# Dividing by the softmax sums after the product with the values, in the last cross attention

## Chip, core and metric

The kernel runs on one core of one Trainium2 chip. The metric is the device time of one execution in microseconds, a median over runs. TensorE (PE in the rows, PEld its weight loads), VectorE (DVE), ScalarE (ACT), GpSimd (POOL) and SyncE (SP) run their own instruction streams and meet through semaphores.

## The reference, cut to what matters

Thirty-two batches of 112 rows of 256 go through four stages: a cross attention, a self attention with routed experts, a second cross attention, and a linear layer on quantised rows. Every stage adds to the residual x. The change lies in the third stage, and the fourth is interleaved with it:

```python
    scale = d ** (-0.5)                      # h, d = 8, 64
    q = (x @ Wq).reshape(B, Sq, h, d).transpose(0, 2, 1, 3)
    k = (context @ Wk).reshape(B, -1, h, d).transpose(0, 2, 1, 3)
    v = (context @ Wv).reshape(B, -1, h, d).transpose(0, 2, 1, 3)
    scores = jnp.einsum('bhid,bhjd->bhij', q, k) * scale
    attn = jax.nn.softmax(scores, axis=-1)
    out = jnp.einsum('bhij,bhjd->bhid', attn, v)
    out = out.transpose(0, 2, 1, 3).reshape(B, Sq, h * d)
    return out @ Wo + bo
...
    x = x + _L1_xattn_ref(_layernorm(x, axis=-1), ctx_768, L1_xattn_Wq, L1_xattn_Wk, L1_xattn_Wv, L1_xattn_Wo, L1_xattn_bo)
    x = x + _L1_ffn_ref(_layernorm(x, axis=-1), L1_ffn_weight, L1_ffn_bias)
```

The context has 375 keys of 192. The softmax divides each row of exponentials by its sum. The linear layer (_L1_ffn_ref) quantises x in blocks of 32 to a small grid before its product.

## The kernel before

The last stage is the function cross_last. It holds one instruction stream per engine, each written as a function step(b, par) that over_batches calls for b from a little below 0 to a little above 31: the first few steps and the last ones are written out, the middle ones are a loop of two steps per turn (TensorE: steps 6 to 29). The order inside a step is written by hand. What an engine does in one step belongs to several batches; `exists` leaves out those that are not there at the two ends.

The eight heads of a batch are four units of two heads. TensorE's step b does, in this order: transposes of the quantised rows xd of batch b-3 (L1984, into a bank of quad) and of the normalised rows xn of batch b+1 (L1984, into proj); scores of units 0 and 1 of batch b (L102); the out product of batch b-2 (L1989, reads oT) and the last linear product of batch b-3 (L1994), both into proj; the transposes of the probabilities of unit 2 of batch b-1 (L108); the query product of batch b+1 (L1969), into the bank that the second head of unit 0's scores held, so that it waits for that unit's exponentials; transposes of unit 3; scores of units 3 and 2; the product of the probabilities with the values of batch b-1 (L114, 48 matrix products of 64 columns of v, output in psum out); then key and value products for the next batches (L182), with the transposes of units 0 and 1 of batch b between them.

VectorE's step b takes the negated maxima of batch b+1 (dve_max, L119) as scores come, adds proj to the residual for batch b-1 (L1899) and to the final rows for batch b-2 (L1910), normalises the four units of probabilities of batch b+1 (dve_normalise, L122 and L126: a reciprocal of two sums, then one multiplication for each of the two heads; units 1 and 0 in mid-step, 3 and 2 at its end), mixes the experts' rows in (L1869), applies the norms (L169), and quantises batch b-1 in twelve instructions from L1302 to L1317, of which the last writes xd.

ScalarE takes exponentials with their sums (act_exp, L134), copies transposed probabilities out of PSUM (act_spread, L130), and copies queries, keys, values, and psum out into oT (L1809). GpSimd subtracts the rounded halves of q, k and the context (L1705, L1708, L1724, L1729, L1735), fetches experts' rows, and computes the norms' powers.

Of the kernel before, what the change touches and what calls it, by code (L numbers as in the profile page):

```python
# [79 lines left out]
class Core:  # L80


    def __init__(self, nc, ctx, name, psum, units, keys, chunk, vdim):
        self.keys, self.chunk, self.chunks, self.vdim = keys, chunk, keys // chunk, vdim
        self.out = psum["out"]
        self.scores = [t[0:T, :, 0:keys] for t in psum["scores"]]
        self.score_sums = [t[0:T, :, 0:keys + 1] for t in psum["scores"]]
        self.turned = psum["turned"][0:chunk, :, 0:self.chunks * T]
        sb = lambda n, shape: ctx.enter_context(nc.sbuf_tensor(f"{name}_{n}", shape, F32))
        sem = lambda n: ctx.enter_context(nc.semaphore(f"{name}_{n}"))  # L90
        self.negmax, self.sums, self.recip = (sb(n, [T, units, 2]) for n in ("negmax", "sums", "recip"))
        self.probs = [sb(f"probs{i}", [T, 2, keys]) for i in range(units)]
        self.probsT = [sb(f"probsT{i}", [chunk, 2, self.chunks, T]) for i in range(units)]
        self.scores_ready, self.max_ready, self.exp_ready = sem("scores_ready"), sem("max_ready"), sem("exp_ready")
        self.recip_ready, self.probs_ready, self.turned_ready = sem("recip_ready"), sem("probs_ready"), sem("turned_ready")
        self.spread_act, self.values_ready = sem("spread_act"), sem("values_ready")
# [24 lines left out]
    def dve_normalise(self, dve, u, done):  # L121
        dve.reciprocal(self.recip[:, u, :], self.sums[:, u, :]).then_inc(self.recip_ready, 1)  # L122
        dve.wait_ge(self.recip_ready, done)
        for j in range(2):
            p = self.probs[u][:, j, :]
            last = dve.tensor_scalar(p, p, self.recip[:, u, j:j + 1], None, ALU.mult)  # L126
        last.then_inc(self.probs_ready, 1)
# [1420 lines left out]
def cross_last(nc, mem, ctx_t, w, residual, out):  # L1548
# [5 lines left out]
    with ExitStack() as ctx:  # L1554
# [70 lines left out]
        def emit(block):  # L1625
# [116 lines left out]
            def _(act):  # L1742
# [3 lines left out]
                def step(b, par):  # L1746
# [11 lines left out]
                    if exists(b):  # L1758
                        act.wait_ge(core.max_ready, 4 * b + 1)
                        wait(act, core.turned_ready, 4 * b - 3)  # L1760
                        core.act_exp(act, 0)
# [20 lines left out]
                    if exists(b):  # L1782
                        act.wait_ge(core.max_ready, 4 * b + 3)
                        wait(act, core.turned_ready, 4 * b)
                        core.act_exp(act, 3)
                    if exists(b + 1):
                        act.wait_ge(k_mm, 4 * b + 5)
                        wait(act, k_ready, 4 * b + 1)
                        act.activation(kT[:, 0, :], psum["turned"][:, 1, :][:, 0:CTXE], ACT.Copy).then_inc(k_whole, 1)
# [16 lines left out]
                    if exists(b - 1):  # L1806
                        act.wait_ge(core.values_ready, 4 * b)
                        wait(act, op_mm, b - 1)
                        act.activation(oT[:, :, :].rearrange("p k t -> p (k t)"), psum["out"][:, 0:4 * T], ACT.Copy).then_inc(o_ready, 1)  # L1809
# [40 lines left out]
            def _(dve):  # L1850
# [37 lines left out]
                def step(b, par):  # L1888
# [14 lines left out]
                    if exists(b + 1):  # L1903
                        dve.wait_ge(core.exp_ready, 4 * b + 6)
                        core.dve_normalise(dve, 1, 4 * b + 5)
# [11 lines left out]
                    if exists(b + 1):  # L1917
                        dve.wait_ge(core.exp_ready, 4 * b + 5)
                        core.dve_normalise(dve, 0, 4 * b + 6)
# [5 lines left out]
                    if exists(b + 3):  # L1925
                        wait(dve, xT_mm, b + 3)
                        norm.dve_apply(dve, b + 3, xn[:, :], row(residual, b + 3))
                    if exists(b - 1):
                        quantise(b - 1, 0)
# [7 lines left out]
                    if exists(b + 1):  # L1937
                        dve.wait_ge(core.exp_ready, 4 * b + 7)
                        core.dve_normalise(dve, 3, 4 * b + 7)
                    if exists(b + 1):  # L1940
                        dve.wait_ge(core.exp_ready, 4 * b + 8)
                        core.dve_normalise(dve, 2, 4 * b + 8)
# [4 lines left out]
            def _(pe):  # L1947
# [49 lines left out]
                def step(b, par):  # L1997
# [67 lines left out]
                    if exists(b - 1):  # L2065
                        pe.wait_ge(core.probs_ready, 4 * b)
# [22 lines left out]
                    if exists(b - 1):  # L2089
                        pe.wait_ge(core.probs_ready, 4 * b - 1)  # L2090
# [54 lines left out]
                    if exists(b - 1):  # L2145
                        pe.wait_ge(core.spread_act, 4 * b)
                        pe.wait_ge(v_ready, 3 * b)
                        core.pe_values(pe, 3, v_of(1 - par))
                    if exists(b + 1):
# [13 lines left out]
                    if exists(b):  # L2163
# [13 lines left out]
                        elif exists(b + 1):  # L2177
                            wait(pe, xT_ready, b + 2)
                        v_product(proj, par, 2)
# [12 lines left out]
                    if exists(b):  # L2192
                        pe.wait_ge(core.probs_ready, 4 * b + 2)
# [25 lines left out]
                    if exists(b):  # L2219
                        pe.wait_ge(core.probs_ready, 4 * b + 1)  # L2220
# [101 lines left out]
```

## Time and profile before

| | us |
|---|---|
| median of 3 runs (1954.52 to 1957.32) | 1955.18 |
| the profiled execution, its own time | 1952.96 |
| its span, first to last instruction | 1951.1 |
| TensorE busy | 1865.6 |
| VectorE busy | 1493.8 |
| ScalarE busy | 1270.0 |
| GpSimd busy | 952.1 |

The span is what the trace covers; 1.9 us of the execution's time lie around it. Busy times are sums over all stages, so the table ranks the engines but doesn't say which of them a given stage waits for. The last stage takes the span from about 1282 us on, some 20 us a batch.

### The profile page before, as it was taken

Reading aid. Unit: us, or ns where it says so; the run is one execution under the profiler, and the core shown is the slowest. Engines: PE = TensorE matmul, PEld = TensorE weight load, DVE = VectorE, ACT = ScalarE, POOL = GpSimd, SP = SyncE. Lnnn points to the kernel's source line nnn. Section 1 sums busy time; section 2 is a strip of 40 time slices with the busy share of each in tenths; the row PEclk is TensorE's granted clock in tenths of the full one; section 3 lists DMA queues with packets and bytes.
Section 4 is the critical chain, followed back from the end, with each engine's and each line's share of the span. In section 5 each row is a group of like instructions: output and inputs, shape, how many; then the busy total and the mean of one; then the engine's idle time right before and its main releaser. Section 6 shows DMA issues by size and latency. Waiting matters only on the chain.

```text
span 1951.1 us, 61515 instructions
## 1 busy us (share of the span) xinstructions
PE 1865.6 (96%) x20887; PEld 1637.1 (84%) x20887; DVE 1493.8 (77%) x3438; ACT 1270.0 (65%) x2720; POOL 952.1 (49%) x1616
## 2 busy tenths in 40 slices
PE   6999999999899999789999999969999999999996
PEld 5888888888678888689999999958888888888885
DVE  6778888788478788766666666657888888888886
ACT  2555555555477777557777777747777677777773
POOL 4556555664256676630000000066767677676751
PEclk8999999999899999899999999979999999999998
DMA  8222233222051111275555655422111111111100
GB/s 238 90 89 88 88 111 95 88 88 63 22 165 33 35 38 40 65 260 190 205 196 188 199 203 189 137 81 60 32 41 35 40 35 40 35 34 38 32 15 10
DMA packets 116595, 182.05 MB, mean 93 GB/s; under 512 B 10850, under 2 KB 94562, under 8 KB 116066
## 3 DMA queue, kind: packets, MB, share of 16 engines
q1 hardware_dynamic: 110386, 166.51, 26.7%
q0 software_dynamic: 6144, 14.69, 2.5%
q8 instruction: 40, 0.66, 0.1%
q14 instruction: 25, 0.20, 0.0%
HBM read 127.68 MB, written 53.48 MB: 93 GB/s over the span
## 4 chain that ended last, share of the span: by engine, by line
PE 52%; DVE 2%; issue 1%; DMA 1%; POOL 1%; ACT 1%; ACTq 0%; SPq 0%; DVEq 0%; POOLq 0%
PE ps_quad L1518 11%; PE ps_out L1538 9%; PE ps_quad L182 6%; PE ps_quad L102 4%; PE ps_out L114 4%; PE ps_turned L108 4%; PE ps_quad L1969 3%; PE ps_proj L1989 3%; PE ps_turned L182 3%; PE ps_proj L182 2%; PE ps_proj L1994 1%; PE ps_proj L1526 1%; DVE c_negmax L119 1%; ACT c_probs L134 0%; DMA c_wv<-in_L_xattn_Wv 0%
## 5 line engine op out<-in xcount | busy, mean ns | idle before, releaser
L1518 PE MATMUL ps_quad<-e_xT,w 128*128 128x128 f32 x2016 | 235.3, 275 | 1.7 <-DVE e_xT L1476 1.7
L1518 PEld LDWEIGHTS ps_quad<-e_xT,w 128*128 128x128 f32 x2016 | 230.4, 192 | 2.2 <-DVE e_xT L1476 2.2
L369 ACT ACTIVATE a_probsT<-ps_quad 125x1792 f32<-125x1792 f32 x96 | 159.9, 1666 | 99.4 <-PE ps_quad L549 99.4
L1658 POOL TENSOR_TENSOR c_held<-minus_half 1x1 f32<-1x1 f32 x32 | 9.5, 298 | 407.9 <-DMA slots<-e_y 405.4
L1433 ACT ACTIVATE e_act_T<-ps_quad,fc_b 128x128 f32<-128x128 f32 x504 | 137.3, 384 | 91.4 <-PE ps_quad L1518 91.3
L134 ACT ACTIVATE c_probs<-ps_quad,c_negmax 112x375 f32<-112x375 f32 x256 | 143.8, 572 | 65.9 <-DVE c_negmax L119 65.9
L1538 PE MATMUL ps_out<-e_w2H,e_aH 128*128 128x256 f32 x504 | 148.4, 294 | 7.3 <-DVE e_w2L L1464 7.2
L126 DVE TENSOR_SCALAR c_probs<-c_probs,c_recip 112x375 f32<-112x375 f32 x256 | 151.0, 631 | 4.5
L1464 DVE TENSOR_TENSOR e_w2L<-w,e_w2H 128x1024 fp32r<-128x1024 f32 x126 | 151.0, 1240 | 0.0
L434 DVE TENSOR_REDUCE a_negmax<-ps_turned 112x2 f32<-112x750 f32 x128 | 120.2, 939 | 34.5 <-PE ps_turned L535 34.3
L119 DVE TENSOR_REDUCE c_negmax<-ps_quad 112x2 f32<-112x750 f32 x128 | 114.0, 931 | 41.2 <-PE ps_quad L102 40.7
L1538 PE MATMUL ps_out<-e_w2L,e_aH 128*128 128x256 f32 x504 | 142.5, 283 | 0.0
L1538 PE MATMUL ps_out<-e_w2H,e_aL 128*128 128x256 f32 x504 | 142.3, 282 | 0.0
L432 DVE TENSOR_REDUCE a_negmax<-ps_quad 112x4 f32<-112x1500 f32 x64 | 110.2, 1722 | 36.4 <-PE ps_quad L535 36.4
L1425 ACT ACTIVATE e_w2H<-w 128x1024 fp32r x126 | 125.3, 1041 | 0.9 <-PE ps_out L1538 0.9
L1484 DVE TENSOR_TENSOR e_y<-ps_out,e_b 128x256 f32<-128x256 f32 x63 | 26.8, 425 | 107.8 <-PE ps_out L1538 107.8
L108 PEld LDWEIGHTS ps_turned<-ident,c_probs 112*125 112x125 f32 x768 | 100.8, 188 | 7.5 <-issue 2.4
L108 PE MATMUL ps_turned<-ident,c_probs 112*125 112x112 f32 x768 | 103.8, 271 | 1.8 <-ACT c_probsT L130 1.8
L1538 PEld LDWEIGHTS ps_out<-e_w2H,e_aH 128*128 128x128 f32 x504 | 96.1, 191 | 10.6 <-issue 6.1
L364 ACT ACTIVATE a_kT<-ps_proj,a_bk 128x376 f32<-128x376 f32 x64 | 36.8, 575 | 101.0 <-PE ps_proj L182 101.0
L130 ACT ACTIVATE c_probsT<-ps_turned 125x672 f32<-125x672 f32 x128 | 95.1, 743 | 10.6 <-PE ps_turned L108 8.2
L1489 DVE TENSOR_TENSOR e_aL<-e_act_T,e_aH 128x1024 fp32r<-128x1024 f32 x63 | 77.2, 1226 | 30.5 <-issue 25.8
(356 smaller groups left out, 6012.8 us busy)
## 6 DMA issues: line engine op xcount, KB each, us to landing
w<-in_fc_t SPq DMA_DIRECT2D x71, 1024.0 KB, 4.9
slots<-a_zeros SPq DMA_DIRECT2D x60, 512.0 KB, 4.9
a_cT<-in_ctx_t SPq DMA_DIRECT2D x32, 375.0 KB, 3.5
c_cT<-in_ctx_t SPq DMA_DIRECT2D x32, 375.0 KB, 3.2
e_xg<-slots SPq DMA_DIRECT2D x63, 128.0 KB, 3.9
slots<-e_y SPq DMA_DIRECT2D x63, 128.0 KB, 1.8
out<-c_fo SPq DMA_DIRECT2D x32, 112.0 KB, 1.9
residual<-in_x SPq DMA_DIRECT2D x1, 2912.0 KB, 19.2
```

Of the source, the lines that this page charges most:

```text
L108: last = pe.transpose(self.turned[:, j, c * T:(c + 1) * T], self.probs[u][:, j, c * self.chunk:(c + 1) * self.chunk], ident[0:T, 0:T])
L119: dve.tensor_reduce(self.negmax[:, u, :], self.scores[u % 2], AX, ALU.max, negate=True).then_inc(self.max_ready, 1)
L126: last = dve.tensor_scalar(p, p, self.recip[:, u, j:j + 1], None, ALU.mult)
L134: last = act.activation(self.probs[u][:, j, :], self.scores[u % 2][:, j, :], ACT.Exp, bias=self.negmax[:, u, j:j + 1], accum_out=self.sums ...
L182: last = pe.matmul(dst, left, right, start=(i == 0), stop=(i == len(terms) - 1))
L369: act.activation(probsT[:, 2 * i:2 * i + 2, :, :].rearrange("p c r x -> p r c x"), quad[0:KC, :, 0:2 * HALF].rearrange("p r (c x) -> p r c ...
L434: dve.tensor_reduce(rows[:, 2 * half:2 * half + 2, 0], plain[0:T, :, 0:CTX], AX, ALU.max, negate=True)\
L1425: act.activation(w2H[:, half * HALF:(half + 1) * HALF], weights_half(e, half), ACT.Copy).then_inc(w2_high, 1)
L1433: last = act.activation(act_T[par][:, c * TILE:(c + 1) * TILE], hidden[par][:, c // 4, (c % 4) * TILE:(c % 4 + 1) * TILE], ACT.Gelu, bias= ...
L1464: dve.tensor_tensor(w2L[:, half * HALF:(half + 1) * HALF], weights_half(e, half), w2H[:, half * HALF:(half + 1) * HALF], ALU.subtract)\
L1518: last = pe.matmul(hidden[par][:, c // 4, (c % 4) * TILE:(c % 4 + 1) * TILE], mem["w1"][:, par, k, c * 128:(c + 1) * 128], xT[par][:, k, : ...
L1538: last = pe.matmul(y_ps[:, 0:D], left[:, rows], right[:, cols], start=(c == 0 and i == 0), stop=(c == NCH - 1 and i == 2))
```

## The change

The probabilities are no longer divided. VectorE takes the eight reciprocals of a batch's sums in one instruction (dve_share), and spreads each over the 64 columns of its head, so that share is 112 rows by four units of 128 columns. TensorE transposes the four blocks into proj (pe_share), after the values' product and ahead of the key products. ScalarE copies them out of PSUM into shareT, in place of its copy of psum out into oT, and at another place in its order. VectorE multiplies psum out with shareT into oT, between applying the norms and quantising. The transposes of the probabilities wait for the exponentials themselves; the product of the values' last chunk, which uses proj too, also waits for ScalarE's copy of shareT. The first exponentials of a batch also wait for the reciprocals of the batch before, since they write the same sums.

```diff
-    def dve_normalise(self, dve, u, done):
-        dve.reciprocal(self.recip[:, u, :], self.sums[:, u, :]).then_inc(self.recip_ready, 1)
+    def pe_share(self, pe, to, ident):
+        for u in range(self.units):
+            last = pe.transpose(to[:, u * T:(u + 1) * T], self.share[:, u, :, :].rearrange("p j d -> p (j d)"), ident[0:T, 0:T])
+        last.then_inc(self.share_mm, 1)
+
+    def dve_share(self, dve, done):
+        dve.reciprocal(self.recip[:, :, :], self.sums[:, :, :]).then_inc(self.recip_ready, 1)
         dve.wait_ge(self.recip_ready, done)
-        for j in range(2):
-            p = self.probs[u][:, j, :]
-            last = dve.tensor_scalar(p, p, self.recip[:, u, j:j + 1], None, ALU.mult)
-        last.then_inc(self.probs_ready, 1)
+        dve.tensor_copy(self.share[:, :, :, :], self.recip[:, :, :].unsqueeze(3).to_broadcast([T, self.units, 2, self.vdim]))\
+           .then_inc(self.share_ready, 1)
...
+                    if exists(b - 1):
+                        act.wait_ge(core.share_mm, b)
+                        wait(act, o_ready, b - 1)
+                        act.activation(core.shareT[:, :, :].rearrange("p u t -> p (u t)"), proj[:, 0:4 * T], ACT.Copy).then_inc(core.share_out, 1)
                     if exists(b + 1):
                         act.wait_ge(k_mm, 4 * b + 5)
...
-                    if exists(b - 1):
-                        act.wait_ge(core.values_ready, 4 * b)
-                        wait(act, op_mm, b - 1)
-                        act.activation(oT[:, :, :].rearrange("p k t -> p (k t)"), psum["out"][:, 0:4 * T], ACT.Copy).then_inc(o_ready, 1)
...
                         norm.dve_apply(dve, b + 3, xn[:, :], row(residual, b + 3))
+                    if exists(b):
+                        dve.wait_ge(core.values_ready, 4 * b + 4)
+                        dve.wait_ge(core.share_out, b + 1)
+                        wait(dve, op_mm, b)
+                        dve.tensor_tensor(oT[:, :, :].rearrange("p k t -> p (k t)"), psum["out"][:, 0:4 * T],
+                                          core.shareT[:, :, :].rearrange("p u t -> p (u t)"), ALU.mult).then_inc(o_ready, 1)
                     if exists(b - 1):
                         quantise(b - 1, 0)
...
                     if exists(b + 1):
-                        dve.wait_ge(core.exp_ready, 4 * b + 7)
-                        core.dve_normalise(dve, 3, 4 * b + 7)
-                    if exists(b + 1):
                         dve.wait_ge(core.exp_ready, 4 * b + 8)
-                        core.dve_normalise(dve, 2, 4 * b + 8)
+                        wait(dve, core.share_mm, b + 1)
+                        core.dve_share(dve, b + 2)
...
                         core.pe_values(pe, 3, v_of(1 - par))
+                    if exists(b - 1):
+                        pe.wait_ge(core.share_ready, b)
+                        if exists(b + 1):
+                            wait(pe, xT_ready, b + 2)
+                        wait(pe, v_ready, 3 * b - 2)
+                        if exists(b - 2):
+                            wait(pe, x_ready, b - 1)
+                        if exists(b - 3):
+                            wait(pe, f_ready, b - 2)
+                        core.pe_share(pe, proj, ident)
...
+                        if exists(b - 1):
+                            pe.wait_ge(core.share_out, b)
                         v_product(proj, par, 2)
```

The other two calls of dve_normalise (units 1 and 0) go without a replacement. Three places show the new order. First, TensorE in its loop, from the values' product on; before:

```order
L2131 REGISTER_ALU
L114 MATMUL ps_out<-c_probsT,c_v 64x112 x24
L2150 ISA
L182 MATMUL ps_turned<-c_cH,c_wkH 128x376
L182 MATMUL ps_turned<-c_cL,c_wkH 128x376
```

and after:

```order
L2135 REGISTER_ALU
L116 MATMUL ps_out<-c_probsT,c_v 64x112 x24
L125 MATMUL ps_proj<-ident,c_share 128x112 x4
L2164 ISA
L187 MATMUL ps_turned<-c_cH,c_wkH 128x376
L187 MATMUL ps_turned<-c_cL,c_wkH 128x376
```

The four transposes of share stand between the values' product and the first key product. Second, VectorE at the end of its loop's second step, from the moments of the next norm to the next step's first maxima (behind the loop's branch); before:

```order
L158 BN_AGGR c_norm_moments<-c_norm_stats 112x2
L122 RECIPROCAL c_recip<-c_sums 112x2
L126 TENSOR_SCALAR c_probs<-c_probs,c_recip 112x375 x2
L122 RECIPROCAL c_recip<-c_sums 112x2
L126 TENSOR_SCALAR c_probs<-c_probs,c_recip 112x375 x2
L61 REGISTER_ALU
L61 COMPARE_AND_BRANCH
L119 TENSOR_REDUCE c_negmax<-ps_quad 112x2 x2
```

and after:

```order
L163 BN_AGGR c_norm_moments<-c_norm_stats 112x2
L129 RECIPROCAL c_recip<-c_sums 112x8
L131 COPY c_share<-c_recip 112x512
L61 REGISTER_ALU
L61 COMPARE_AND_BRANCH
L121 TENSOR_REDUCE c_negmax<-ps_quad 112x2 x2
```

Two reciprocals and four multiplications ahead of the maxima became one reciprocal and one copy. Third, VectorE near the end of the program, in the step that quantises batch 30; before:

```order
L158 BN_AGGR c_norm_f_moments<-c_norm_f_stats 112x2
L1910 TENSOR_TENSOR c_fo<-ps_proj,c_xf 112x256
L169 TENSOR_SCALAR c_xq<-residual,c_norm_f_moments,c_norm_f_rstd 112x256
L1302 TENSOR_REDUCE c_mx_scale<-c_xq 112x8
L1303 TENSOR_SCALAR c_mx_scale<-c_mx_scale 112x8
```

and after:

```order
L163 BN_AGGR c_norm_f_moments<-c_norm_f_stats 112x2
L1913 TENSOR_TENSOR c_fo<-ps_proj,c_xf 112x256
L174 TENSOR_SCALAR c_xq<-residual,c_norm_f_moments,c_norm_f_rstd 112x256
L1932 TENSOR_TENSOR c_oT<-ps_out,c_shareT 128x448
L1307 TENSOR_REDUCE c_mx_scale<-c_xq 112x8
L1308 TENSOR_SCALAR c_mx_scale<-c_mx_scale 112x8
```

The product into oT, for batch 31, stands ahead of the first quantising instruction.

## Rows read from the trace of the kernel before

**Rows 1.** Page, part 1: busy us, share of the span, instructions.

```profile
PE 1865.6 (96%) x20887; PEld 1637.1 (84%) x20887; DVE 1493.8 (77%) x3438; ACT 1270.0 (65%) x2720; POOL 952.1 (49%) x1616
```

**Rows 2.** Windows: us, busy PE, PEld, DVE, ACT, POOL (instructions), PEclk, DMA share, GB/s.

```profile
1600.00:1700.00 100.00, 97.86 (x814) 87.13 (x814) 88.85 (x215) 70.78 (x179) 70.19 (x110) 1.00 0.13 36
```

**Rows 3.** Chain that ended last, 1255 to 1420: start us, us, what.

```profile
1313.38 2.01 PE ps_quad L1969 x16
...
1355.34 2.45 PE ps_out L114 x48
...
1374.96 2.45 PE ps_out L114 x48
...
1394.50 2.45 PE ps_out L114 x48
1396.95 1.93 PE ps_turned L182 x10
...
1405.43 0.19 PE ps_quad L1984 x2
...
1408.82 0.86 DVE c_negmax L119
...
1411.14 2.01 PE ps_quad L1969 x16
...
1415.03 2.45 PE ps_out L114 x48
```

**Rows 4.** TensorE's waits, 1280 to the end: us in total, times, longest us.

```profile
PE ps_quad L1969 <- ACT c_probs L134: 9.4, 13, 1.0
```

**Rows 5.** Timeline of VectorE, two steps: start us, us, what [idle before <-releaser].

```profile
1607.72 1.47 DVE L126 TENSOR_SCALAR c_probs<-c_probs,c_recip 112x375 f32<-112x375 f32 x2
...
1627.82 0.74 DVE L126 TENSOR_SCALAR c_probs<-c_probs,c_recip 112x375 f32<-112x375 f32 x2
1628.47 1.78 DVE L119 TENSOR_REDUCE c_negmax<-ps_quad 112x2 f32<-112x750 f32 x2
```

**Rows 6.** Timeline of TensorE, the second of these two steps.

```profile
1626.10 0.35 PE L1984 MATMUL ps_quad<-ident,c_xd 112*128 112x112 f32 x2
...
1631.12 1.95 PE L1969 MATMUL ps_quad<-c_xT,c_wq 128*128 128x112 f32 x16
```

**Rows 7.** Timeline of GpSimd, the first of these two steps.

```profile
1607.93 1.04 POOL L1705 TENSOR_TENSOR c_kL<-c_kT,c_kH 128x376 fp32r<-128x376 f32 x1 [0.54 <-ACT c_kH L1757]
```

**Rows 8.** Page, part 5: groups by line: busy us, mean ns | idle before.

```profile
L126 DVE TENSOR_SCALAR c_probs<-c_probs,c_recip 112x375 f32<-112x375 f32 x256 | 151.0, 631 | 4.5
...
L108 PE MATMUL ps_turned<-ident,c_probs 112*125 112x112 f32 x768 | 103.8, 271 | 1.8 <-ACT c_probsT L130 1.8
```

**Rows 9.** Timeline of VectorE, end of the stage of the experts.

```profile
1270.89 0.68 DVE L1305 TENSOR_TENSOR e_mx_t<-e_wf,e_mx_inv 128x512 f32<-128x512 f32 x1
```

**Rows 10.** Timeline of VectorE, the end of the program.

```profile
1916.38 0.42 DVE L1302 TENSOR_REDUCE c_mx_scale<-c_xq 112x8 f32<-112x256 f32 x1
...
1924.73 0.42 DVE L1899 TENSOR_TENSOR residual<-ps_proj,c_xb 112x256 f32<-112x256 f32 x1 [1.45 <-PE ps_proj L1989]
...
1927.36 0.42 DVE L1302 TENSOR_REDUCE c_mx_scale<-c_xq 112x8 f32<-112x256 f32 x1
```

**Rows 11.** Timeline of ScalarE, in the loop.

```profile
1622.21 0.54 ACT L1809 ACTIVATE c_oT<-ps_out 128x448 f32<-128x448 f32 x1
```

**Rows 12.** Timeline of TensorE, the end of the program.

```profile
1913.80 2.52 PE L114 MATMUL ps_out<-c_probsT,c_v 125*64 125x112 f32 x48
1916.25 0.49 PE L182 MATMUL ps_proj<-c_wvH,c_cH 128*125 128x512 f32 x1
...
1927.00 2.52 PE L114 MATMUL ps_out<-c_probsT,c_v 125*64 125x112 f32 x48
1932.61 0.64 PE L1984 MATMUL ps_quad<-ident,c_xd 112*128 112x112 f32 x2 [3.09 <-DVE c_xd L1317]
```

More of the change, by code:

```diff
@@ L91, in __init__ @@
         self.negmax, self.sums, self.recip = (sb(n, [T, units, 2]) for n in ("negmax", "sums", "recip"))
+        self.share, self.shareT, self.units = sb("share", [T, units, 2, vdim]), sb("shareT", [128, units, T]), units
         self.probs = [sb(f"probs{i}", [T, 2, keys]) for i in range(units)]
@@ L94, in __init__ @@
         self.scores_ready, self.max_ready, self.exp_ready = sem("scores_ready"), sem("max_ready"), sem("exp_ready")
-        self.recip_ready, self.probs_ready, self.turned_ready = sem("recip_ready"), sem("probs_ready"), sem("turned_ready")
+        self.recip_ready, self.share_ready, self.turned_ready = sem("recip_ready"), sem("share_ready"), sem("turned_ready")
+        self.share_mm, self.share_out = sem("share_mm"), sem("share_out")
         self.spread_act, self.values_ready = sem("spread_act"), sem("values_ready")
@@ L1760, in step @@
                         wait(act, core.turned_ready, 4 * b - 3)
+                        wait(act, core.recip_ready, b)
                         core.act_exp(act, 0)
@@ L1902, in step @@
                         norm_f.dve_moments(dve, b - 1, row(residual, b - 1))
-                    if exists(b + 1):
-                        dve.wait_ge(core.exp_ready, 4 * b + 6)
-                        core.dve_normalise(dve, 1, 4 * b + 5)
                     if exists(b - 2):
@@ L1916, in step @@
                         core.dve_max(dve, 2)
-                    if exists(b + 1):
-                        dve.wait_ge(core.exp_ready, 4 * b + 5)
-                        core.dve_normalise(dve, 0, 4 * b + 6)
                     if exists(b + 4):
@@ L1937, in step @@
                     if exists(b + 1):
-                        dve.wait_ge(core.exp_ready, 4 * b + 7)
-                        core.dve_normalise(dve, 3, 4 * b + 7)
-                    if exists(b + 1):
                         dve.wait_ge(core.exp_ready, 4 * b + 8)
-                        core.dve_normalise(dve, 2, 4 * b + 8)
+                        wait(dve, core.share_mm, b + 1)
+                        core.dve_share(dve, b + 2)
                 over_batches(dve, step, 4, 2, 4, 4)
@@ L2065, in step @@
                     if exists(b - 1):
-                        pe.wait_ge(core.probs_ready, 4 * b)
+                        pe.wait_ge(core.exp_ready, 4 * b)
                         if exists(b - 1):
@@ L2089, in step @@
                     if exists(b - 1):
-                        pe.wait_ge(core.probs_ready, 4 * b - 1)
+                        pe.wait_ge(core.exp_ready, 4 * b - 1)
                         if exists(b - 1):
@@ L2192, in step @@
                     if exists(b):
-                        pe.wait_ge(core.probs_ready, 4 * b + 2)
+                        pe.wait_ge(core.exp_ready, 4 * b + 1)
                         if exists(b + 1):
@@ L2219, in step @@
                     if exists(b):
-                        pe.wait_ge(core.probs_ready, 4 * b + 1)
+                        pe.wait_ge(core.exp_ready, 4 * b + 2)
                         if exists(b):
```

## The prediction

> **What bounds the kernel now.** I read the page first: TensorE is busy for 96% of the span and VectorE for 77% [rows 1]. A share says nothing of one stage, so I then looked at a stretch of the last cross attention: TensorE 97.86 us of 100 at the full granted clock, VectorE 88.85 [rows 2]. Then the chain that ended last. It runs along TensorE, step after step, and leaves it at one place only: in front of the query product (L1969) it goes over VectorE's negated maximum (L119) and ScalarE's exponentials to TensorE again [rows 3]. The first row of the values' product (L114) marks a step: from 1355.34 to 1374.96 a step lasts 19.62 us, the one from 1394.50 to 1415.03 lasts 20.53 us. So a step with the hole costs 0.91 us more. The view of TensorE's waits counts 13 such holes, 9.4 us of idle time together [rows 4]. They sit in every second step from 1411.14 on (12 of them, 40.07 us apart), and one stands at 1313.38, right at the start [rows 3].
>
> Why every second step: in the hole's step the maximum starts some 3.4 us after the step's first transpose (1405.43 to 1408.82) [rows 3], because the normalising before it is slow. One pair of multiplications over the probabilities took 1.47 us there, and 0.74 us in the step after it, where the maximum starts at 1628.47, 2.37 us after the step's start at 1626.10, and the query product goes ahead without idling, 5.02 us after that start [rows 5, 6]. GpSimd was at work on kL during the slow pair [rows 7].
>
> **The change, part by part.** All of it is in the last stage; ahead of it nothing moves.
>
> *VectorE.* A step loses eight multiplications over 112x375 (mean 631 ns, 5.0 us a step [rows 8]) and four reciprocals. It gains one reciprocal of eight columns, a copy that spreads them over 512, and a product of 448 columns out of PSUM. For the product the nearest rows are 0.68 us for 512 columns out of SBUF [rows 9] and 0.42 us for 256 out of PSUM [rows 10]; between them, nearer to the larger, I take 0.62 us. For the copy the same rows bound it: 0.4 to 0.7 us. So VectorE loses over 3 us a step. That is worth only what the hole is worth, since TensorE waits for VectorE nowhere else in the loop.
>
> *The hole goes.* After the change, what stands between the quantising and the next maximum is the moments, a reciprocal and the copy: about 0.6 + 0.2 + 0.7 = 1.5 us. The quantising itself starts later, behind the new product. In the step of 1415.03: values end at 1417.48, the four transposes 0.38, their last result 0.16 later (two of them are recorded as 0.35 us [rows 6] but advance the chain by 0.19 [rows 3]), the copy on ScalarE 0.54 [rows 11], the product 0.62, and two handoffs that I take at 0.05 each: 1419.28. It lasts about 5.2 us where nothing disturbs it (1927.36 to the transposes of its result at 1932.61 [rows 10, 12]); I allow 1 us for disturbance, so it ends by 1425.5. The next step of TensorE starts at 1415.03 + 10.93 (1394.50 to 1405.43) + 0.38 = 1426.34, so the transposes of its result find it done with 0.8 us to spare. The maximum can then start by 1427.0, and with another 1 us of trouble at 1428.0, 1.7 us after the step's start; 2.37 us was early enough [rows 5, 6]. I count all twelve holes as gone: 12 x 0.91 = **-10.9 us** (bounds: 12 x 0.72 of pure idle time, and nothing). The one at 1313.38 stays: there TensorE has too little work between scores and query product, and VectorE isn't late.
>
> *TensorE gains four transposes a step*, of 112x128 against the identity, in front of the key products, and TensorE is the bound, so nothing hides them. The nearest row is the same shape: two transposes in 0.19 us [rows 3], hence 0.38 us for four. Lower bound: the values' 48 products pass in 2.45 us, 0.05 each, so 0.20. Upper bound: the transposes open with five waits (share_ready, xT_ready, v_ready, x_ready, f_ready), all for things done long before; should they make TensorE run dry once, a restart as at the hole is added, 0.91 less the mean idle time of 9.4 / 13 = 0.72, so 0.19, and 0.57 in all. I take 0.38, the identical shape. Thirty full steps carry it (steps 1 to 30; the last two are in the tail): 30 x 0.38 = **+11.4 us** (6.0 to 17.1).
>
> The Trainium skill, "TensorE: Matmul & The Clock Gate", section "Part 4: PE-mode transpose", puts a transpose inside a kernel at about 275 ns; taken as occupancy that would be 1.1 us a step and 33 us in all. The trace has that figure as one instruction's duration, 271 ns [rows 8], but shows six of them advancing faster than that; it stands below as a rival.
>
> *ScalarE* swaps the copy of oT for the copy of shareT, the same 128x448 out of PSUM, 0.54 us [rows 11]. It stands earlier, behind the third exponential, where ScalarE waits for the key product anyway: nothing in the loop. In proj, the product of the values' last chunk now also waits for this copy; in the loop two key products (1.93 us [rows 3]) lie between and cover it.
>
> *The tail loses.* VectorE's new product stands between applying the norm and quantising. In the loop that is covered; at the end it isn't. Before, quantising of batch 29 started at 1916.38 and of batch 30 at 1927.36, the latter while TensorE still multiplied values (from 1927.00) [rows 10, 12]. TensorE then idled until 1932.61 for that quantised block, since its transposes stand ahead of the last out product. After the change both quantisings wait for values, transposes, ScalarE's copy and the product. Batch 29: values end at 1916.25, + 0.38 + 0.16 + 0.54 + 0.62 + 0.10 = 1918.05 in place of 1916.38, +1.67. Everything behind it shifts by that: values of batch 31 end at 1927.00 + 2.45 + 1.67 = 1931.12, + 1.80 = 1932.92 in place of 1927.36: +5.56. From there the order is the old one, one instruction waiting for another to the end. **+5.6 us** (5 to 7; the granted clock dips in that idle time, and may dip longer).
>
> Sum on the profiled execution: 1952.96 - 10.9 + 11.4 + 5.6 = 1959.1 us. The median of the runs shown lies 2.2 us above the profiled one, so I say 1955.2 + 6.1 = **1961.3 us**. With the lower bounds 6.0 - 10.9 + 5 it is 1955.3, with the upper ones 17.1 - 10.9 + 7 it is 1968.4.
>
> **The rivals.**
> (a) *The transposes cost less than their row*: no gain, no loss. TensorE loses time anyway where it leaves the values' half-width products, and part of the four may go there. At 0.20 us each step: +6.0 - 10.9 + 5.6 = +0.7, 1955.9 us. It decides below 0.30 us a step, where the sum is under +3.9. Against it: TensorE's stream is dense there.
> (b) *Faster*: the tail's +5.6 doesn't come because TensorE's chain there hides it, and the transposes cost 0.20: -4.9, 1950.3 us. It needs the out product of batch 31 to get ahead of the transposes of batch 30, and the order is fixed; little speaks for it.
> (c) *The holes stay.* The spreading copy, or what is behind it, meets GpSimd's work as the normalising did (1.47 for 0.74), and the maximum is late still: +11.4 + 5.6 = +17.0, 1972.2 us. It decides when the maximum starts more than about 2.4 us after the step's start. Against it: only one instruction of this kind is left, where there were four pairs. The Trainium skill, "SBUF — State Buffer", section "Who interferes with whom", says that copies and scalar operations of VectorE may take a port pair shared with GpSimd for a whole instruction; the pair of 1.47 us beside GpSimd's work agrees with that.
> (d) *The new waits show*: 0.57 us a step, +17.1 - 10.9 + 5.6 = +11.8, 1967.0 us.
> (e) *Transposes run one after another*, each for its recorded 271 ns [rows 8]: 4 x 0.271 x 30 = 32.5, so +27.2, 1982.4 us. Six of the same kind in the trace speak against it.
>
> **How the numbers follow.** Forecast (transposes 0.30 to 0.48 us a step, holes gone, tail +5 to +7): 0.55, its own range 1958 to 1966. (a) 0.22, (b) 0.06, (c) 0.06, (d) 0.09, (e) 0.02. A measurement can tell 0.2%, 3.9 us, from no change: slower begins at 1959.1. Of the forecast some nine tenths lie above. Slower: 0.50 + 0.06 + 0.09 + 0.02 = 0.67; same: 0.22 + 0.05 = 0.27; faster: 0.06. The range goes from (a), 1955.5, to above (d), 1970.0, and leaves out (b), (c), (e) and the edges.
>
> **What would show it.** In the trace of after: no wait of the query product for ScalarE's exponentials from the sixth step on; values to values 20.0 us in all steps alike (19.6 + 0.38) instead of 19.6 and 20.5; four transposes in about 0.38 us in front of the key products; at the end an idle time of TensorE ahead of the transposes of batch 30 of over 6 us, where it was 3.09 [rows 12]. I'd be wrong if steps last under 19.9 us (a), if the hole stands at its old place (c), if they last over 20.1 us (d), or if the stretch from the last batch's scores to the end isn't 5 to 7 us longer.

## Result and the profile after

| us | before | after |
|---|---|---|
| median | 1955.18 | 1960.47 |
| the profiled execution | 1952.96 | 1959.58 |
| its span | 1951.1 | 1957.7 |
| first to 31st values' product (L114, after: L116), 30 steps | 596.60 | 595.46 |
| values of batch 30 to the end | 37.30 | 44.05 |

The ratio of after to before is 1.0033, with a 95% interval of 1.0025 to 1.0041: 5 to 8 us slower. Forecast were 1961.3 us, from 1955.5 to 1970.0. Three differences make up the 6.6 us between the spans. The first values' product starts 0.99 us later (1317.20, now 1318.19); the 30 steps up to the 31st (batch 30) give back 1.14; the end costs 6.75. The 0.99 aren't the change's: the query product ahead of it starts 1.00 us later already (1313.38, now 1314.38), and in the runs below the first values' product starts anywhere between 1317 and 1322 us. One execution of e2 (2294.98 us) and one of e6 (6887.55 us) lie far above their others, and the ratios leave them out.

The page's first part, and the same 100 us of the loop as in [rows 1, 2]:

```profile
PE 1871.8 (96%) x21015; PEld 1646.2 (84%) x21015; DVE 1383.8 (71%) x3150; ACT 1281.7 (65%) x2720; POOL 938.8 (48%) x1616
```

```profile
1600.00:1700.00 100.00, 100.00 (x839) 89.67 (x838) 70.53 (x172) 74.01 (x182) 68.67 (x110) 1.00 0.13 36
```

VectorE lost 18 us of work in 100, and TensorE, which had 2 us of holes there, has none. The waits of TensorE in the last stage (total us, times, longest) answer to [rows 4]:

```profile
PE ps_quad L1988 <- DVE c_xd L1322: 15.7, 3, 8.0
...
PE ps_quad L1973 <- ACT c_probs L139: 1.0, 1, 1.0
PE ps_proj L187 <- ACT c_shareT L1795: 0.7, 1, 0.7
```

Of 13 waits of the query product (now L1973) one is left, the one near the start. TensorE waits once for the copied share, 0.7 us, at the end. The chain that ended last, two steps of it (start us, us, what; [rows 3]):

```profile
1357.03 2.45 PE ps_out L116 x48
1359.48 0.53 PE ps_proj L125 x4
...
1376.95 2.45 PE ps_out L116 x48
...
1396.82 2.45 PE ps_out L116 x48
```

Steps of 19.92 and 19.87 us; two steps take 39.8 us where they took 40.07. At the end of the program, TensorE's timeline ([rows 12]) and VectorE's ([rows 10]):

```profile
1913.65 2.52 PE L116 MATMUL ps_out<-c_probsT,c_v 125*64 125x112 f32 x48
1916.11 0.60 PE L125 MATMUL ps_proj<-ident,c_share 112*128 112x112 f32 x4
...
1928.63 2.52 PE L116 MATMUL ps_out<-c_probsT,c_v 125*64 125x112 f32 x48
1931.09 0.60 PE L125 MATMUL ps_proj<-ident,c_share 112*128 112x112 f32 x4
1938.62 0.64 PE L1988 MATMUL ps_quad<-ident,c_xd 112*128 112x112 f32 x2 [6.93 <-DVE c_xd L1322]
1939.05 3.62 PE L1993 MATMUL ps_proj<-c_wo,c_oT 128*112 128x256 f32 x8
```

```profile
1917.49 0.62 DVE L1932 TENSOR_TENSOR c_oT<-ps_out,c_shareT 128x448 f32<-128x448 f32 x1 [2.13 <-ACT c_shareT L1795]
1918.03 0.41 DVE L1307 TENSOR_REDUCE c_mx_scale<-c_xq 112x8 f32<-112x256 f32 x1
...
1932.84 0.62 DVE L1932 TENSOR_TENSOR c_oT<-ps_out,c_shareT 128x448 f32<-128x448 f32 x1 [3.89 <-ACT c_shareT L1795]
1933.38 0.41 DVE L1307 TENSOR_REDUCE c_mx_scale<-c_xq 112x8 f32<-112x256 f32 x1
```

VectorE idles 3.89 us ahead of the product, with the quantising behind it, and TensorE idles 6.93 us for that quantised block, where it was 3.09.

### The profile page after: what moved, and what is told of

It is laid out like the page before. It is cut to its first block, busy times and chain, and to the rows that moved or that the text cites. A ratio compares the mean times of both kernels' runs of the same rounds, so it can differ in the third digit from the quotient of the medians.

```text
span 1957.7 us, 61715 instructions
## 1 busy us (share of the span) xinstructions
PE 1871.8 (96%) x21015; PEld 1646.2 (84%) x21015; DVE 1383.8 (71%) x3150; ACT 1281.7 (65%) x2720; POOL 938.8 (48%) x1616
## 4 chain that ended last, share of the span: by engine, by line
PE 53%; DVE 1%; DMA 1%; POOL 1%; issue 1%; ACT 0%; SPq 0%; ACTq 0%; DVEq 0%; POOLq 0%
PE ps_quad L1523 11%; PE ps_out L1543 9%; PE ps_quad L187 6%; PE ps_turned L110 4%; PE ps_out L116 4%; PE ps_quad L104 4%; PE ps_proj L1993 3%; PE ps_quad L1973 3%; PE ps_turned L187 3%; PE ps_proj L187 2%; PE ps_proj L1998 1%; PE ps_proj L125 1%; PE ps_proj L1531 1%; DMA c_wv<-in_L_xattn_Wv 0%; PE ps_quad L1988 0%
## 5 line engine op out<-in xcount | busy, mean ns | idle before, releaser
L1543 PEld LDWEIGHTS ps_out<-e_w2L,e_aH 128*128 128x128 f32 x504 | 97.0, 192 | 0.0
```

The source lines that it names most:

```text
L1543: last = pe.matmul(y_ps[:, 0:D], left[:, rows], right[:, cols], start=(c == 0 and i == 0), stop=(c == NCH - 1 and i == 2))
```

## Experiments

Times in the table are medians; ratios are to the kernel before, run on the same chip. "Two steps" is the time from one values' product to the next but one, in the middle of the loop.

| run | median us | ratio, 95% interval | two steps, us |
|---|---|---|---|
| e1_product_behind | 1955.7 | 1.0005, 0.9995 to 1.0014 | 39.82 |
| e2_one_turn | 1954.25 | 0.9996, 0.9987 to 1.0005 | 39.29 |
| e3_max_first | 1965.22 | 1.0058, 1.0045 to 1.0071 | 40.28 |
| e4_before_turns | 1956.1 | 0.9998, 0.9989 to 1.0008 | 39.84 |
| e5_no_division | 1944.42 | 0.9947, 0.9934 to 0.9960 | 39.17 |
| e6_maxima_first | 1945.69 | 0.9947, 0.9933 to 0.9961 | 39.17 |
| e7_before_one_turn | 1946.84 | 0.9955, 0.9942 to 0.9968 | 39.21 |
| e8_narrow_pool | 1946.26 | 0.9953, 0.9939 to 0.9967 | 39.10 |
| e9_turns_at_start | 1957.24 | 1.0012, 1.0000 to 1.0023 | 40.08 |
| e10_out_first | 1940.87 | 0.9920, 0.9907 to 0.9934 | 39.17 |

### The end: the product behind the quantising (on the kernel after)

```diff
-                    if exists(b):
-                        dve.wait_ge(core.values_ready, 4 * b + 4)
-                        ...  (the product into oT)
                     if exists(b - 1):
                         quantise(b - 1, 2)
+                    if exists(b):
+                        dve.wait_ge(core.values_ready, 4 * b + 4)
+                        ...
```

> The changed kernel with one move: VectorE's product into oT stands behind the quantising of batch b-1, in every step, where the change puts it ahead. My theory: the change's loss at the end (values of batch 31 to the end: 24.0 us before, 28.9 after, and 14.98 for 13.21 us between the values of batches 30 and 31) comes from the quantising that waits for values, transposes, copy and product. Then the quantising of batch 30 starts near its old place, some 5.3 us earlier, and the last out product waits some 0.3 us for the product: 1955 us, ratio to before 1.000; the loop's steps keep their 19.9 us. Rival: the extra time is that of the chain values, transposes, copy, product, out product itself, which the move leaves in place: 1960 us, ratio 1.003.

Measured: 1955.7 us, the loop as after, and from the values of batch 30 to the end 38.4 us (1915.46 to 1953.9) in place of 44.05. TensorE's end:

```profile
1929.41 2.52 PE L116 MATMUL ps_out<-c_probsT,c_v 125*64 125x112 f32 x48
...
1935.03 0.41 PE L1988 MATMUL ps_quad<-ident,c_xd 112*128 112x112 f32 x2 [2.57 <-DVE c_xd L1322]
1935.56 3.54 PE L1993 MATMUL ps_proj<-c_wo,c_oT 128*112 128x256 f32 x8
```

From the values of batch 31 to the transposes 5.62 us, as before (5.61), for 9.99 after. The loss at the end is the order of two things on VectorE, and this run removes 5.6 of its 6.75 us.

### Four idle transposes, divisions kept (on the kernel before)

```diff
+                    if exists(b - 1):
+                        ...  (the waits for proj, as the change has them)
+                        for u in range(4):
+                            pe.transpose(proj[:, u * T:(u + 1) * T], ident[0:T, :], ident[0:T, 0:T])
                     if exists(b + 1):
                         pe.wait_ge(c_split, 2 * b + 4)
```

> The kernel before with four transposes of 112x128 into proj at the place where the change has them (of a constant tile, read by nobody; nothing else changes, the divisions stay). Theory of the sum: the transposes and the holes are separate terms, 30 x 0.34 = +10.2 us: 1965.4 us, holes unchanged. Rival: in two steps TensorE needs 2 x 19.89 = 39.78 us and the pair lasts 40.08 with the hole, so the hole shrinks by what TensorE gains in work, and the pair stays at 40.08: +0.5 us, 1955.7 us. Then the 10.9 us that the change takes away by removing the holes and the 11.4 us that it adds were partly the same time.

Measured: 1956.1 us; 128 transposes that nobody reads (four for each batch) cost nothing that these runs can tell (0.9989 to 1.0008). The rival held, and more than it said, since the two steps became shorter (39.84 for 40.08). TensorE's waits:

```profile
PE ps_quad L1969 <- ACT c_probs L134: 1.0, 1, 1.0
```

All twelve holes of the loop are gone with VectorE's divisions still there. So the transposes and the holes aren't separate terms.

### One transpose in place of four, with VectorE light and heavy

On the kernel after, with three blocks of share not transposed from step 6 on (ScalarE's copy of share also scales by 2.0 ** -12):

```diff
-        for u in range(self.units):
+        for u in range(blocks):
             ...
-                        core.pe_share(pe, proj, ident)
+                        core.pe_share(pe, proj, ident, 4 if isinstance(b, int) and b < 6 else 1)
```

> The changed kernel with one transpose of share instead of four from step 6 on (three of the four blocks are left out, so shareT holds other values there, scaled down; every other instruction stays). My theory: each transpose in the stream costs TensorE its 0.095 us, so 26 steps lose 3 x 0.095 each: -7.4 us against the changed kernel, 1953 us, and a step lasts 19.6 us. Rival: what a step pays (0.34 us) is the entry into another kind of product and the waits ahead of it, once per step whatever the number: 1960 us, steps of 19.9 us.

Measured: 1954.25 us, 0.37% less than after by the two ratios (some 7 us), steps of 19.60 and 19.69 us. The price goes by the number for the three left out: (39.82 - 39.29) / 6 = 0.088 us each. On the kernel before, one idle transpose a step from step 6 on in place of e4's four (the diff is against e4):

```diff
-                        for u in range(4):
+                        for u in range(4 if isinstance(b, int) and b < 6 else 1):
                             pe.transpose(proj[:, u * T:(u + 1) * T], ident[0:T, :], ident[0:T, 0:T])
```

> The kernel before with one idle transpose a step (four up to step 5) where the run with four had four; VectorE's divisions stay. It stands to the changed kernel with one transpose as the run with four idle ones stands to the changed kernel: the same TensorE work with the heavy VectorE. Theory A: at 0.1 us more a step VectorE still falls behind by some 0.25 us a step, so holes remain, the mean step is near 19.9 to 20.0 us: 1953 to 1956 us. Theory B: any shift of TensorE against GpSimd's work is enough to end the holes, steps of 19.65 us, 1946 to 1948 us.

Measured: 1946.84 us, 0.45% **faster** than the kernel before, by adding work to the engine that bounds it. Theory B. Steps of 19.58 and 19.63 us, and one hole left, at the start. VectorE's timeline in a step of the loop of before that has a hole, with one subtraction of GpSimd in its place:

```profile
1599.52 1.00 POOL L1729 TENSOR_TENSOR c_kL<-c_kT,c_kH 128x376 fp32r<-128x376 f32 x1 [2.39 <-ACT c_kH L1793]
1599.56 0.99 DVE L1303 TENSOR_SCALAR c_mx_scale<-c_mx_scale 112x8 f32<-112x8 f32 x1
...
1605.77 1.84 DVE L126 TENSOR_SCALAR c_probs<-c_probs,c_recip 112x375 f32<-112x375 f32 x2
...
1609.11 1.77 DVE L119 TENSOR_REDUCE c_negmax<-ps_quad 112x2 f32<-112x750 f32 x2
```

and the same place with one idle transpose, where L1303 and the second pair are this short in every step of the loop:

```profile
1600.99 0.17 DVE L1303 TENSOR_SCALAR c_mx_scale<-c_mx_scale 112x8 f32<-112x8 f32 x1
1601.01 1.01 POOL L1729 TENSOR_TENSOR c_kL<-c_kT,c_kH 128x376 fp32r<-128x376 f32 x1 [2.45 <-ACT c_kH L1793]
1601.43 0.87 DVE L1305 TENSOR_TENSOR c_mx_t<-c_xq,c_mx_inv 112x256 f32<-112x256 f32 x1
...
1606.84 1.83 DVE L126 TENSOR_SCALAR c_probs<-c_probs,c_recip 112x375 f32<-112x375 f32 x2
...
1608.78 0.74 DVE L126 TENSOR_SCALAR c_probs<-c_probs,c_recip 112x375 f32<-112x375 f32 x2
1609.43 1.78 DVE L119 TENSOR_REDUCE c_negmax<-ps_quad 112x2 f32<-112x750 f32 x2
```

The small multiplication takes 0.17 us for 0.99; the subtraction, now just behind it, makes L1305 longer instead (0.87, for 0.42 in the step of before), so that this place saves 0.37 us. The second pair takes 0.74 for 1.47 [rows 5]. Together that is 1.1 us, and the maximum starts 2.36 us after the step's first transpose (1607.07) instead of 3.48 (1605.63).

### The lightening alone (on the kernel before)

```diff
-        for j in range(2):
-            p = self.probs[u][:, j, :]
-            last = dve.tensor_scalar(p, p, self.recip[:, u, j:j + 1], None, ALU.mult)
-        last.then_inc(self.probs_ready, 1)
+        dve.tensor_scalar(self.probs[u][:, 0, 0:1], self.probs[u][:, 0, 0:1], self.recip[:, u, 0:1], None, ALU.mult).then_inc(self.probs_ready, 1)
```

> The kernel before with the multiplications of the probabilities left out (per unit one multiplication of a single column stays, so the result isn't divided); no transposes of share, no product, ScalarE's copy into oT as before. It is the change's lightening of VectorE alone. Theory A, the prediction's: the holes are VectorE's lateness, and go with its work: all steps 19.55 us, 12 x 0.98 = -11.8 us, 1943.4 us. Theory B, after the run with four idle transposes, in which the holes went with VectorE's work untouched: what removes them is TensorE's longer step, and without it they stay: 1955 us.

Measured: 1944.42 us, no hole in the loop, theory A as far as it goes: less work on VectorE is enough. With the run before it follows that it isn't needed. The six cases side by side, two steps in us:

| transposes of this kind a step | divisions on VectorE | without them |
|---|---|---|
| 0 | 40.08 (before) | 39.17 (e5) |
| 1 | 39.21 (e7) | 39.29 (e2) |
| 4 | 39.84 (e4) | 39.82 (after) |

Only in the first row does VectorE's work matter.

### What makes the pairs slow, and how the holes return

GpSimd's four subtractions for kL cut to 8 columns in the loop of the kernel before (one of the four is shown):

```diff
+                    w = CTXE if isinstance(b, int) else 8
...
-                        pool.tensor_tensor(kL[1 - par][:, 3, :], kT[:, 3, :], kH[1 - par][:, 3, :], ALU.subtract)
+                        pool.tensor_tensor(kL[1 - par][:, 3, 0:w], kT[:, 3, 0:w], kH[1 - par][:, 3, 0:w], ALU.subtract)
```

> The kernel before with GpSimd's four subtractions for kL cut from 376 to 8 columns inside the loop (steps written out keep them whole), so the low halves of k are partly stale there; all else stays. Theory: VectorE's pairs of multiplications take 1.47 to 1.84 us in place of 0.74 because GpSimd's subtractions run beside them; without those the pairs take 0.74, the first maximum comes in time in every step, the holes go: 1943.4 us. Rival: the slow pairs have another cause (ScalarE's accesses to the same tiles, or VectorE itself) and stay, with the holes: 1955 us.

Measured: 1946.26 us, and one hole in the whole loop instead of twelve. By itself that could be one more shift, like the idle transpose. But the one hole left stands where the subtractions are whole again: GpSimd's written-out steps with them begin at 1821.93, and in the second of these a pair is slow again and TensorE waits (VectorE, GpSimd, TensorE):

```profile
1841.44 1.47 DVE L126 TENSOR_SCALAR c_probs<-c_probs,c_recip 112x375 f32<-112x375 f32 x2
1841.66 1.04 POOL L1706 TENSOR_TENSOR c_kL<-c_kT,c_kH 128x376 fp32r<-128x376 f32 x1 [0.54 <-ACT c_kH L1758]
1845.24 2.01 PE L1970 MATMUL ps_quad<-c_xT,c_wq 128*128 128x112 f32 x16 [0.69 <-ACT c_probs L134]
```

So the holes hang on GpSimd's subtractions beside VectorE's work. The pairs didn't all become fast; the mean multiplication (busy us, mean ns, over the same 380 us) fell from the first row, before, to the second:

```profile
L126 DVE TENSOR_SCALAR c_probs<-c_probs,c_recip 112x375 f32<-112x375 f32 x152 | 93.6, 656 | 2.7
```

```profile
L126 DVE TENSOR_SCALAR c_probs<-c_probs,c_recip 112x375 f32<-112x375 f32 x155 | 85.0, 590 | 2.8
```

GpSimd's other work (the context's halves, L1671, and the residual with its bias, L1717 and L1722) still runs beside some of them. The four idle transposes of e4 in steps 1 to 5 only:

```diff
-                    if exists(b - 1):
+                    if isinstance(b, int) and 1 <= b < 6:
                         ...
                         for u in range(4):
                             pe.transpose(proj[:, u * T:(u + 1) * T], ident[0:T, :], ident[0:T, 0:T])
```

> The kernel before with four idle transposes in steps 1 to 5 only, none in the loop. The run with one idle transpose a step lost its holes; this one asks why. Theory A: the holes are a state that VectorE and GpSimd fall into and stay in; a shift of TensorE at the start puts the collisions elsewhere for good, no holes, 1.7 us for the 20 transposes: 1946 us. Theory B: at TensorE's undisturbed pace of 19.55 to 19.62 us VectorE falls behind until it collides, so the holes come back within a few steps of the loop, every second step: 1953 to 1956 us; then it is the 0.1 us in each step that kept them away.

Measured: 1957.24 us, and the query product waits twelve times again, eleven of them in the loop; steps of 19.55 and 20.53 us from the sixth on. Theory B: the 0.1 us has to be there in each step. The traces show what it decides. In before, between 1400 and 1900 us, the subtraction L1729 starts 0.02 to 0.06 us ahead of the small multiplication L1303 in twelve steps; L1303 then takes 0.97 to 1.00 us, the second pair of the step 1.47, and these twelve are the steps with a hole. In the others it starts 0.19 us or more behind L1303, and there is no hole. The same goes for the eleven holes here and for the one of e8. With one idle transpose the subtraction starts 0.01 us or more behind L1303 in every step. Why the order alternates from step to step was not followed further.

### A way without the change: the maxima first (on the kernel before)

First only the maximum of unit 0 was moved, between the two normalisations at the end of a step (unit 2's first):

```diff
-                        dve.wait_ge(core.scores_ready, 4 * b + 5)
-                        core.dve_max(dve, 0)
...
                     if exists(b + 1):
-                        dve.wait_ge(core.exp_ready, 4 * b + 7)
-                        core.dve_normalise(dve, 3, 4 * b + 7)
+                        dve.wait_ge(core.exp_ready, 4 * b + 8)
+                        core.dve_normalise(dve, 2, 4 * b + 7)
+                    if exists(b + 2):
+                        dve.wait_ge(core.scores_ready, 4 * b + 9)
+                        core.dve_max(dve, 0)
                     if exists(b + 1):
-                        dve.wait_ge(core.exp_ready, 4 * b + 8)
-                        core.dve_normalise(dve, 2, 4 * b + 8)
+                        core.dve_normalise(dve, 3, 4 * b + 8)
```

TensorE's waits for the probabilities of units 2 and 3 change places to match, here and in e6 (not shown).

> The kernel before with VectorE's end of a step in another order: normalise unit 2, then the negated maximum of the next batch's unit 0, then normalise unit 3 (before: normalise 3, normalise 2, maximum 0); the probabilities are divided as before. My theory: the hole in every second step is only the lateness of that one maximum, behind two slow pairs of multiplications; then the query product never waits, all steps last 19.55 us as the undisturbed ones do, 12 x 0.98 = -11.8 us, 1943.4 us, with no change of the arithmetic. Rival: VectorE has too much work in those steps, so the lateness moves to the next thing that TensorE needs of it (the transposes of the probabilities, the last scores' maxima): 1952 to 1956 us.

Measured: 1965.22 us, slower than both kernels. The query product's holes went, but TensorE got a new wait in every step:

```profile
PE ps_turned L108 <- ACT c_probsT L130: 15.7, 32, 1.9
```

ScalarE's timeline shows where it is from: the second exponentials, ahead of the copy in ScalarE's order, wait for the maximum that stands behind unit 3's divisions.

```profile
1620.62 0.57 ACT L134 ACTIVATE c_probs<-ps_quad,c_negmax 112x375 f32<-112x375 f32 x1 [1.23 <-DVE c_negmax L119]
...
1621.73 0.73 ACT L130 ACTIVATE c_probsT<-ps_turned 125x672 f32<-125x672 f32 x1
```

Then both maxima went ahead of unit 3's divisions (against before; their old places at the start of the step go, not shown):

```diff
                     if exists(b + 1):
-                        dve.wait_ge(core.exp_ready, 4 * b + 7)
-                        core.dve_normalise(dve, 3, 4 * b + 7)
+                        dve.wait_ge(core.exp_ready, 4 * b + 8)
+                        core.dve_normalise(dve, 2, 4 * b + 7)
+                    if exists(b + 2):
+                        dve.wait_ge(core.scores_ready, 4 * b + 9)
+                        core.dve_max(dve, 0)
+                    if exists(b + 2):
+                        dve.wait_ge(core.scores_ready, 4 * b + 10)
+                        core.dve_max(dve, 1)
                     if exists(b + 1):
-                        dve.wait_ge(core.exp_ready, 4 * b + 8)
-                        core.dve_normalise(dve, 2, 4 * b + 8)
+                        core.dve_normalise(dve, 3, 4 * b + 8)
```

> The kernel before with VectorE's end of a step reordered: normalise 2, then both maxima of the next batch's units 0 and 1, then normalise 3. In the run with only the first maximum moved TensorE waited 0.5 us in each step ahead of the transposes of unit 3, for ScalarE, which stood at the second exponentials and came late to the copy of unit 2's transposed probabilities. Theory: with both maxima ahead of normalise 3 that wait is gone too, no holes, steps of 19.55 us: 1943.4 us, faster than both kernels. Rival: unit 3's probabilities now come too late for their transposes, some 7 us after the step's start; 1955 us or more.

Measured: 1945.69 us, as the theory had it, with all the divisions in place and slow pairs too (1.84 and 1.71 us in one step). Unit 2's, the 1.84, still stands ahead of the maxima, which start 1.89 us after the step's first transpose (1606.64 and 1604.75); unit 3's, the 1.71, now lies behind them, where TensorE shows no wait for it. Last, TensorE's order near the end on top of it:

```diff
-                    if exists(b - 3):
+                    if exists(b - 3) and not (isinstance(b, int) and b == NB + 1):
                         pe.wait_ge(xd_ready, b - 2)
...
                         out_product(proj)
+                    if isinstance(b, int) and b == NB + 1:
+                        pe.wait_ge(xd_ready, b - 2)
+                        wait(pe, xdT_ready, b - 3)
+                        turn_rows(psum["quad"][:, 3, :], xd, xdT_mm)
```

> The order with both maxima ahead of normalise 3, and in the last step but one TensorE's out product of batch 31 ahead of the transposes of batch 30's quantised rows. The prediction held that this order is why a late quantising of batch 30 delays the end, and why TensorE idles 3.09 us there in the kernel before. Theory: the out product then runs within that idle time, and VectorE's addition to the residual waits for the last product of batch 30 alone, some 2.5 us earlier: 1942 us. Rival: the chain through quantising, transposes, copy and last product of batch 30 ends as late as before, within 0.5 us: 1944.5 us.

Measured: 1940.87 us, ratio 0.992, faster than both kernels. TensorE's end:

```profile
1920.68 2.52 PE L114 MATMUL ps_out<-c_probsT,c_v 125*64 125x112 f32 x48
1923.84 1.98 PE L1988 MATMUL ps_proj<-c_wo,c_oT 128*112 128x256 f32 x8 [0.64 <-ACT c_oT L1809]
1926.28 0.41 PE L1983 MATMUL ps_quad<-ident,c_xd 112*128 112x112 f32 x2 [0.46 <-DVE c_xd L1317]
```

The out product runs in the former idle time, and from these values to the end it is 21.5 us (1920.68 to 1942.2) for 24.1 before. That is 2.6 us; the medians lie 4.8 apart, more than the trace explains.

## Why the prediction was right, point by point

The median moved by 5.3 us for 6.1 forecast. That it came so near is partly luck: the steps came 1.6 us below the sum of their two terms, the end 1.15 above its own. The sum's bounds also kept the holes at -10.9, though the working bounds them by 8.6 and nothing; it didn't matter here.

- **The transposes** (forecast 0.38 us a step, 0.20 to 0.57). Against the loop without holes (39.17 for two steps) the change's 39.82 is 0.325 us a step, 9.8 us in all for 11.4. In front of the key products the row held: the first of these starts 2.82 us after the values do, for 2.45 before, so 0.37 for the four. Some 0.05 comes back behind that place, 0.02 of it in the first key product (0.26 us to the second, for 0.28), a little of what rival (a) had. Each of the last three costs 0.088 (e2). The recorded duration, the base of rival (e), is no price: 4 x 0.271 would have been 1.08 a step. That figure, near the 275 ns of the Trainium skill's "TensorE: Matmul & The Clock Gate", "Part 4: PE-mode transpose", isn't what a transpose in a stream costs here.
- **The holes** (-10.9). Twelve went and the one at the start stayed, as forecast; from 40.08 to 39.17 for two steps, twelve times, is 10.9. Their sum with the transposes was forecast at +0.5 and measured at -1.14 from the first to the 31st values' product.
- **The cause of it** is the step that failed, though the sum held. The prediction let the lighter VectorE remove the holes, and had the transposes fully paid, since "nothing hides them". Either of the two alone removes the holes (e5; e4 and e7), and with four transposes the lighter VectorE is worth nothing in the loop (39.84 and 39.82). Taken in the order lightening, then transposes, the two terms are right; taken the other way round the first is -0.24 for two steps and the second nothing.
- **The collision with GpSimd** as what makes VectorE late: shown by e8, so far as the four subtractions go, and by which of L1729 and L1303 starts first in each step. It agrees with the Trainium skill, "SBUF — State Buffer", "Who interferes with whom", which also says that an instruction of VectorE with two inputs in SBUF contends with GpSimd's reads: the changed kernel's L1310 takes 1.09 to 1.27 us in the loop, started inside a subtraction in each step, and 0.42 at the end.
- **VectorE's new rows**: product 0.62 us (forecast 0.62), copy 0.71 in the loop (0.4 to 0.7), the maximum 1.3 us after the step's first transpose (1628.16 and 1626.86; forecast 1.7 at worst); the quantising ends 0.9 us ahead of its transposes (0.8).
- **The tail** (+5.6, bounds 5 to 7; measured +6.75). Up to the values of batch 31 +1.78 (forecast 1.67); from there to the transposes +4.38 (forecast 3.89); from there to the end +0.59, forecast as a chance of the clock only. The 0.49 above the forecast is the handoff from ScalarE's copy to VectorE's product: taken at 0.05 us, it lasted 0.58 there. The granted clock was 0.63 between 1935 and 1940 and 0.68 in the next 5 us, between the two levels' 0.5 and 1.0, so that TensorE ran at the lower one for part of the time; the out product, 1.89 us for batch 30, took 3.62 there and 3.33 in the same place before, and the linear product behind it 1.38 for 1.03; these two make up the 0.59. Since e1 gives 5.6 of the 6.75 back, the order on VectorE is the cause of these. Most of the rest is the 0.7 us wait for the copied share, which e1 keeps (13.95 us between the values of batches 30 and 31, for 13.20 before).

Rivals (a) to (e): the transposes' 0.325 us a step lies above the 0.30 below which (a) decides, though the steps, 19.91 us in the mean, lie nearer to the 19.9 below which it was to hold than to the 20.0 forecast; (b) needed an end that hides, and it didn't; (c) and (d) would have shown as waits, and the one new wait is 0.7 us; (e) is answered above.

## What to carry to other kernels

A hole that comes from two engines colliding can be removed by an edit that shifts one of them a little in every step (a shift at the start alone, e9, did nothing), so before crediting its removal to an edit's purpose, make the edit's side effect alone: here idle transposes on the engine that bounds the kernel did the same. Where a wait comes from the order within one engine's stream, look for what is urgent there before cutting work; two maxima moved ahead of a division gave more than removing all divisions by way of transposes. And at the end of a program a new instruction ahead of an old chain can cost all that it waits for: here 5.6 us, which the other order of two things on VectorE gives back.

## What the runs showed of the hardware

- An instruction of VectorE on 112x8 elements, 0.17 us by itself, took 0.99 us when it started with a subtraction of GpSimd (1599.56 and 1599.52 in the trace of before). Its length says little about what a collision costs. Reciprocals (0.13 and 0.20 us) and the maxima (1.77 us for two) that started inside the same kind of subtraction kept their length.
- After ScalarE's copy VectorE's product starts 0.20 us behind the copy's end for batch 30 (1917.29, 1917.49), but 0.58 us for batch 31 (1932.26, 1932.84), with VectorE idle ahead of both; e2 has the same 0.20 and 0.58. No row shows what holds it; this stays open.
